# GpSimd's loop over edge gathers written out, with the index column read straight from the table

## The reference: a graph layer and a routed feed-forward layer

```python
def gnn(features):                       # features = layernorm(x)
    msgs = features[src] * edge_weight[:, None]
    agg = segment_sum(msgs, dst, 12500)  # dst is sorted
    return agg @ W.T + b
def ffn(xf):                             # xf = layernorm(x)
    H = gelu(xf @ W1 + b1)               # 256 -> 1024
    probs = softmax(H @ Wg + bg)         # 8 experts, the best one is taken
    e = argmax(probs)
    return probs[e] * (H @ Wd[e] + bd[e])
x = x + gnn(layernorm(x))
x = x + ffn(layernorm(x))
```

## Time and profile before

| | |
|---|---|
| device time, median of 3 | 3712.2 us (3704.54 to 3714.25) |
| span of the profiled execution | 2829.9 us |
| own device time of the profiled execution | not recorded; the median is 882.3 us above the span |
| GpSimd busy | 1869.4 us, 66% of the span |
| TensorE busy | 1998.5 us, 71% (its mean granted clock is 0.746 of full) |
| VectorE busy | 1162.7 us, 41% |
| edge gathers (line 404) | 1664, from 77 us to 2206 us |
| routed stage | from about 2350 us to the end |

### The profile page before, as it was taken

How to read it: one execution, slowest core, us unless ns; L and a number is a source line. 1 busy time by engine, 2 the same in 40 slices (tenths; PEclk the granted TensorE clock), 3 DMA queues, 4 the chain that set the end, 5 groups by cost and what they waited for, 6 DMA issues and landing times.

```text
span 2829.9 us, 41767 instructions
## 1 busy us (share of the span) xinstructions
PE 1998.5 (71%) x10526; PEld 1297.4 (46%) x10527; DVE 1162.7 (41%) x3507; ACT 444.5 (16%) x847; POOL 1869.4 (66%) x2093
## 2 busy tenths in 40 slices
PE   0245776766767667677667677666776768999998
PEld 0123443443434334344334343433443447888887
DVE  8532443434434334344344344343443464333332
ACT  7000011000110000110001110001100112344342
POOL 0777777777777777777777777777777103555553
PEclk9955677666766666766666766667766889999999
DMA  9433444344444444444444444444434253555553
GB/s 389 151 102 119 147 147 136 119 142 147 147 147 118 132 148 148 148 139 122 138 148 147 147 126 123 148 147 148 146 118 131 85 183 127 179 184 178 181 185 126
DMA packets 153586, 420.21 MB, mean 148 GB/s; under 512 B 33320, under 2 KB 67499, under 8 KB 150880
## 3 DMA queue, kind: packets, MB, share of 16 engines
q0 software_dynamic: 100032, 300.27, 35.1%
q1 hardware_dynamic: 53536, 119.73, 11.3%
HBM read 328.02 MB, written 92.82 MB: 149 GB/s over the span
## 4 chain that ended last, share of the span: by engine, by line
POOL 51%; PE 23%; issue 17%; DVE 4%; DMA 2%; POOLq 1%; DVEq 1%; ACT 0%; ACTq 0%
POOL big L404 51%; PE psA L660 3%; PE psG L660 3%; PE psE L660 3%; PE psH L660 3%; PE psH L579 2%; DMA big<-xn_table,stage 1%; PE psR L521 1%; DVE stats L716 1%; PE psE L529 1%; PE psH L650 1%; POOL stage L387 1%; PE psE L650 1%; PE psA L650 1%; PE psG L521 1%
## 5 line engine op out<-in xcount | busy, mean ns | idle before, releaser
L404 POOL DMA_INDIRECT big<-xn_table,stage x1664 | 1613.6, 970 | 492.9 <-issue 470.4
L529 PEld LDWEIGHTS psE<-place,parts 128*128 128x128 f32 x1664 | 369.5, 318 | 385.5 <-DVE parts L875 220.2
L521 PE MATMUL psR<-big,sel_narrow 128*32 128x256 f32 x1664 | 215.9, 610 | 448.0 <-DMA big<-xn_table,stage 256.3
L529 PE MATMUL psE<-place,parts 128*128 128x64 f32 x1664 | 428.1, 423 | 139.0 <-DVE parts L875 139.0
L579 PE MATMUL psH<-xn2T,w 128*128 128x512 f32 x800 | 403.8, 663 | 63.2 <-issue 62.5
L472 ACT ACTIVATE hidT<-psH,b 128x512 f32<-128x512 f32 x200 | 137.5, 688 | 1656.6 <-PE psH L579 1656.6
L579 PEld LDWEIGHTS psH<-xn2T,w 128*128 128x128 f32 x800 | 169.3, 215 | 267.3 <-issue 265.1
L521 PEld LDWEIGHTS psR<-big,sel_narrow 128*32 128x32 f32 x1664 | 41.5, 137 | 481.8 <-issue 469.5
L886 DVE TENSOR_TENSOR place<-iota,shift_f 128x256 f32<-128x256 f32 x104 | 44.2, 425 | 466.1 <-issue 466.1
L521 PE MATMUL psG<-big,sel_narrow 128*32 128x256 f32 x1664 | 214.1, 604 | 0.0
L882 DVE TENSOR_TENSOR big<-psE,big 128x128 f32 x416 | 121.5, 292 | 188.0 <-PE psE L529 188.0
(11 more groups left out here) (195 smaller groups left out, 2272.8 us busy)
## 6 DMA issues: line engine op xcount, KB each, us to landing
row_table<-rows SPq DMA_DIRECT2D x25, 2064.0 KB, 8.0
big<-xn_table,stage POOLq DMA_INDIRECT x1664
big<-in_x SPq DMA_DIRECT2D x10, 1280.0 KB, 17.4
xn_table<-big SPq DMA_DIRECT2D x10, 1280.0 KB, 13.3
big<-in_x SPq DMA_DIRECT2D x25, 512.0 KB
row_table<-big SPq DMA_DIRECT2D x25, 512.0 KB, 3.9
big<-in_Wd SPq DMA_DIRECT2D x8, 1024.0 KB, 12.0
hidT<-in_dstT SPq DMA_DIRECT2D x2, 840.0 KB, 30.5
```

Source lines behind the costliest of these rows:

```text
L404: nc.gpsimd.indirect_dma_start(out=xring[:, h * STEP_TILES + j, :], out_offset=None, in_=xn_dram[:, :], in_offset=bass.IndirectOffsetOnAxi ...
L521: mm = nc.tensor.matmul(psQ[q % 2][j * LANES:(j + 1) * LANES, 0:C], sel_narrow[:, t, :], xring[:, t, :], start=True, stop=True)
L529: mm = nc.tensor.matmul(psE[q % 2][:, k * NARROW:(k + 1) * NARROW], parts[:, q % 2, k * P:(k + 1) * P], place[:, q, :], start=True, stop=True)
```

## The change

The staging copies, the waits that protect `stage`, the wait for the copy and the semaphore instructions after the waits are gone from the edge stage. All 104 sections are written out one behind the other, without a loop. Each gather reads its column of `src_i` at an address fixed when the program is built. The two waits on `s_edge_mm` stay at the same places with the same values. `stage` itself stays, since the routed stage uses it.

```diff
-            def stage_indices(g, h, uses):
-                if uses is not None:
-                    pool.wait_ge(s_gath[h], uses * (STEP_TILES * 16))
-                    pool.sem_inc(s_pass, 1)
-                nc.gpsimd.tensor_copy(stage[:, h, :],
-                                      src_i[:, bass.ds(g * STEP_TILES, STEP_TILES)]).then_inc(s_staged, 1)
-            def gather_section(g, h, turn):
-                pool.wait_ge(s_edge_mm, g * STEP_TILES + STEP_TILES // 2)
-                pool.sem_inc(s_pass, 1)
-                pool.wait_ge(s_staged, g + 1)
-                pool.sem_inc(s_pass, 1)
+            def gather_section(g):
+                h = g % SECTIONS
                 for j in range(STEP_TILES):
-                    if j == STEP_TILES // 2:
-                        uses = turn + (h + 1) // SECTIONS
-                        stage_indices(g + 1, (h + 1) % SECTIONS, None if isinstance(g, int) and g < SECTIONS - 1 else uses)
-                        pool.wait_ge(s_edge_mm, g * STEP_TILES + STEP_TILES)
-                        pool.sem_inc(s_pass, 1)
+                    if j % (STEP_TILES // 2) == 0:
+                        pool.wait_ge(s_edge_mm, g * STEP_TILES + STEP_TILES // 2 + j)
                     nc.gpsimd.indirect_dma_start(
                         out=xring[:, h * STEP_TILES + j, :], out_offset=None, in_=xn_dram[:, :],
-                        in_offset=bass.IndirectOffsetOnAxis(ap=stage[:, h, j:j + 1], axis=0)
+                        in_offset=bass.IndirectOffsetOnAxis(
+                            ap=src_i[:, g * STEP_TILES + j:g * STEP_TILES + j + 1], axis=0)
                     ).then_inc(s_gath[h], 16)
-            stage_indices(0, 0, None)
-            for h in range(SECTIONS):
-                gather_section(h, h, 0)
-            with pool.Fori(1, NG // SECTIONS) as i:
-                for h in range(SECTIONS):
-                    gather_section(i * SECTIONS + h, h, i)
-            for g in range(NG // SECTIONS * SECTIONS, NG):
-                gather_section(g, g % SECTIONS, g // SECTIONS)
+            for g in range(NG):
+                gather_section(g)
```

## The result

The kernel after took 3676.69 us in the median of four executions (3657.72 to 3686.61), the kernel before 3713.22 beside it: a ratio of 0.9883 (95% interval 0.9858 to 0.9908), or 36.5 us less. The larger surprise is the span. The profiled execution of the kernel after spans 3684.6 us of a time of 3686.61, so 2 us lie around it, not 882. The profile of before, with its 2829.9 us, thus showed a kind of execution that the timed ones in this comparison were not. In all later sessions, on three chips, the kernel before took 2831 to 2835 us in the median, with 2 us around its span.

The account below looks back on a forecast made before the run. GpSimd's list of gathers was taken to bound the edge stage. Savings of 9.2 + 2.4 + 1.0 = 12.6 us were subtracted from the median 3712.2, giving 3699.6 us, range 3690 to 3735.

Parts of the forecast that it names:

- The 882.3 us around the span: Difference between the median 3712.2 and the profiled span 2829.9 us, taken as lying outside the trace and held fixed.
- GpSimd waits for nobody in the edge stage: Edge stage: GpSimd issues one gather each 1.25 us without waiting for other engines, so its list sets the stage's length.
- the sum of 12.6 us: Whole kernel: 9.2 for copies, 2.4 for gathers behind them and 1.0 for the first gather, subtracted from the median.
- What bounds the kernel: Edge stage: GpSimd's list of 1664 gathers sets the pace, so time saved per gather or copy comes off the end.
- Staging copies, 9.2 us: GpSimd's list in the edge stage: each of 104 copies costs 0.393 less the usual gap of 0.305, 0.088 us.
- The gather behind a copy, 2.4 us: Edge stage: the gather following each of 104 copies takes 0.023 us longer, which should go with the copy.
- the pace is taken back: Rival, edge stage: other engines' rhythm holds gathers up and eats the saving; 3711 us, no change that shows; chance 0.14.
- The first gather, 1.0 us: Start of the edge stage: without the first copy the first gather starts 1.0 us sooner, at most 1.12.
- Waits, semaphore instructions, loop, fetches: GpSimd, edge stage: removing waits, semaphore instructions and loop register work saves 0; fetching the written-out code costs 0.
- The rival of stalls on fetches: GpSimd runs dry fetching written-out code once in eight sections, 2.87 us each: 37.3 us more, 3736.9; chance 0.13.
- the rival of a dearer table: Edge gathers reading indices from `src_i` are slower than from `stage`: up to +126 us, half the bound 3763; chance 0.03.
- the rival that more goes than the copies: Edge gathers: hold-ups that come with the loop or copies vanish too, 38 us more saved, 3661 us; chance 0.05.

Follow-up runs that it names:

- direct_pass: Kernel after with a semaphore instruction put back behind each of GpSimd's two waits per section; 2820.24, 2824.94 and 2820.26 us.
- staged_written_out: Kernel before with only the loop written out, staging copies, their waits and semaphore instructions kept; 2833.78 and 2832.76 us, ratios 1.0003 and 1.0004.

## Why the prediction was wrong

**The 882.3 us around the span: the step that failed.** "I hold these 882.3 us fixed and subtract from the median" read two different kinds of execution as one execution and its surroundings. With 2 us around the span in every later run, the median and the span could not belong to the same behaviour. With it fell "GpSimd waits for nobody in the edge stage" as a statement on the timed executions: it was true of the profiled one, but in the first comparison's trace of the kernel after GpSimd waits 879.3 us for TensorE or "remote", and it is at 0% of the chain, where the earlier trace rows had 51%. For before in that comparison there is no trace; that its edge stage was longer in the same way is inferred from its time alone. That the first comparison moved in the forecast's direction is therefore no support for the sum of 12.6 us.

**What bounds the kernel: right where increments are prompt.** GpSimd's list sets the edge stage there. Four copies a section lengthen the list by 35.1 us and the time by 34.2.

**Staging copies, 9.2 us: right in kind, a little large.** 0.083 us a copy, 8.6 us for 104, by the runs with unread copies; the prediction had 0.088. Its 17.7 / 104 took in the 0.92 us in front of the very first gather, which it counted again in a term of its own; without it the gap is (17.7 - 0.92) / 103 = 0.163, and a copy costs 0.223 + 0.163 - 0.305 = 0.081. That a copy costs less than half of its own duration is confirmed.

**The gather behind a copy, 2.4 us: not found.** That gather is slower (0.97), but the sum of the gathers' times does not fall when the copies go: 1613.6 us in the mean of the traces with and without. Those traces differ among themselves by more than 2.4 us, so a small gain cannot be excluded. It may be that it is lost among the gathers that something else holds up, which would be the rival "the pace is taken back" in a small dose; that is not shown.

**The first gather, 1.0 us: 0.4.** The gather starts 0.4 us sooner than in the earlier trace rows and not 1.1, so most of the gap behind the first copy is there without the copy too.

**Waits, semaphore instructions, loop, fetches: 0, right.** direct_pass and staged_written_out show it each by itself. (The code that is new to GpSimd is 96 sections and not 101, as eight were passed once before too: three, the loop's three, two.) The rival of stalls on fetches, the rival of a dearer table (946 ns) and the rival that more goes than the copies are all out in the ordinary case.

The sum with measured terms is 8.6 + 0 + 0.4 = 9.0 us; measured are 8.0, 9.7 and 9.1.

**The 36.5 us of the first comparison: open.** Shown is that late increments were there in the kernel after, for the copies counted above only where GpSimd was issuing gathers, and that the time is in the waits. Not shown is what makes them late, and which part of the change gave 36.5 us. The chip of that comparison is not on record, and neither it nor the recording of the trace, which lost most of its semaphore updates there, was tried as a cause. A full ring as such, the written-out form as such and the semaphore instructions as such are each without such an effect in ordinary sessions, and with late increments none of them could be tried, as no later session had them. It may be that with late increments anything that GpSimd leaves out counts more; that is a guess and not a finding.

## What to carry to other kernels

Before a single profile is used to price a change, its span is held against the median of the timed executions; where other executions leave 2 us between the two, as here, a gap of hundreds says that the profile is of another behaviour, and then it bounds nothing. A small operation between two instructions with a fixed gap is priced by the difference of the rhythm across it (here 0.083 us for a copy of 0.22), not by its duration. A saving that is read off a slower neighbour counts only when a sum over all instances shows it; here it did not.

## What was not expected of the hardware

- The same two kernels ran at 3713 and 3677 us in one comparison and at 2834 and 2825 in three others. In the long form, 130 of VectorE's 416 copies wait 1.0 to 19.8 us on semaphores whose matmuls are listed as done, all of them while GpSimd issues indirect DMAs, and in the ordinary one none waits over 0.08.
- An indirect gather of 128 rows took GpSimd 967 ns in the mean with 1 KB rows and 963 ns with 256 B rows, and two gathers stand 0.30 us apart with the loop or without it, and with or without the waits (once met) and semaphore instructions between them.
- Eight times the matmuls of line 521 brought TensorE 1678.0 us of issue in front of that line, in 125 stretches, against 191.8 us in 71 in the kernel before. That is 13.4 us in the mean instead of 2.7, while the longest hardly differs, 25.3 and 24.7. The cause was not tried.
